# GpSimd rounds and clips half of w2, VectorE lowers it, and the orders of four engines are written anew

## The reference, cut to what matters

```python
w_down = down_project * dg[:, None] + db[:, None]        # dg, db, ug, ub from cond_512
act = relu(x @ w_down)                                    # 256 -> 64
y = act @ (up_project * ug[:, None] + ub[:, None]) + x    # 64 -> 256, the adapter's output
def bitlinear(x, w, b): return act_quant(rmsnorm(x)) @ weight_quant(w).T + b
out = x + bitlinear(gelu(bitlinear(y, w1, b1)), w2, b2)   # 256 -> 1024 -> 256
# weight_quant: s = 1 / clip(mean|w|); clip(round(w * s), -1, 1) / s
# act_quant:    s = 127 / clip(max|x|); clip(round(x * s), -128, 127) / s
```

## Time and profile before

| what | value |
|---|---|
| time, median of 3 runs | 84.02 us (83.64 to 84.12) |
| the profiled execution's own time | 84.57 us |
| its span, first to last instruction | 82.9 us |
| around the span | 1.67 us |
| granted TensorE clock | 1.0 of full speed |
| busy time, share of the span: PE | 68.6 us, 83% |
| VectorE | 71.6 us, 86% |
| ScalarE | 65.3 us, 79% |
| GpSimd | 44.1 us, 53% |

### The profile page before, as it was taken

One profiled execution on the slowest core, in us unless ns is written; L12 is line 12 of the kernel. 1 busy time (PEld: TensorE's weight loads), 2 busy tenths in 40 slices (PEclk: granted clock), 3 DMA queues, 4 the chain that ended last, 5 costly groups with the idle time before them and its releaser, 6 DMA issues.

```text
span 82.9 us, 1692 instructions
## 1 busy us (share of the span) xinstructions
PE 68.6 (83%) x507; PEld 39.9 (48%) x507; DVE 71.6 (86%) x153; ACT 65.3 (79%) x127; POOL 44.1 (53%) x113
## 2 busy tenths in 40 slices
PE   4989717599799449899999999999999999948740
PEld 1533215034354134376666594484765662836730
DVE  2158859999899999999999999989999989999950
ACT  0601198838899997969999999999999999999600
POOL 6800007856459989970078183079604872975140
PEclk9999999999999999999999999999999999999999
DMA  0887999999300000000030200300030030002033
GB/s 26 260 296 265 405 342 425 427 415 382 125 4 4 0 12 0 4 0 0 0 126 9 116 11 0 127 0 8 0 127 0 0 127 0 12 21 106 0 127 127
DMA packets 3212, 9.18 MB, mean 111 GB/s; under 512 B 370, under 2 KB 882, under 8 KB 2820
## 3 DMA queue, kind: packets, MB, share of 16 engines
q1 hardware_dynamic: 3168, 9.05, 28.9%
q10 hardware_dynamic: 36, 0.04, 0.1%
HBM read 6.98 MB, written 2.10 MB: 110 GB/s over the span
## 4 chain that ended last, share of the span: by engine, by line
PE 42%; DVE 23%; DMA 10%; issue 8%; POOL 6%; ACT 4%; SPq 3%; DVEq 1%; POOLq 0%; ACTq 0%
PE out_ps L347 11%; DMA w<-w_t 10%; PE h L309 10%; DVE mx L650 7%; PE q2t_ps L333 6%; PE up_ps L279 5%; PE h L316 4%; DVE q L691 4%; DVE w2q L823 2%; POOL rms L1024 2%; PE out_ps L345 2%; PE q2t_ps L290 2%; DVE step L659 2%; DVE y L738 2%; DVE mx L655 2%
## 5 line engine op out<-in xcount | busy, mean ns | idle before, releaser
L650 DVE TENSOR_REDUCE mx<-g 128x1 f32<-128x1024 f32 x16 | 19.4, 1210 | 0.5 <-ACT g L513 0.3
L513 ACT ACTIVATE g<-h,deq 128x1024 f32<-128x1024 f32 x16 | 18.2, 1137 | 0.2 <-PE h L316 0.2
L521 ACT ACTIVATE junk<-g,sq_scale 128x1024 bf16<-128x1024 f32 x15 | 17.5, 1172 | 0.0
L309 PE MATMUL h<-w1q,q1t 128*128 128x512 f16 x64 | 16.0, 380 | 1.5 <-ACT q1t L537 1.5
L347 PE MATMUL out_ps<-w2q,q2t 128*128 128x256 f16 x112 | 14.4, 273 | 0.0
L691 DVE TENSOR_SCALAR q<-g,m 128x1024 f32<-128x1024 f32 (+1 forms) x16 | 13.1, 825 | 0.1
L1009 POOL TENSOR_TENSOR var<-ms,eps_w 128x2 f32<-128x2 f32 (+1 forms) x10 | 2.8, 278 | 19.4 <-ACT junk_y L531 10.1
L347 PEld LDWEIGHTS out_ps<-w2q,q2t 128*128 128x128 f16 x112 | 10.9, 98 | 1.6 <-issue 0.3
L993 POOL TENSOR_TENSOR xx<-xx,b 128x512 f32<-128x512 f32 x8 | 10.1, 1273 | 1.7 <-DMA b<-b_rows 1.6
L548 ACT ACTIVATE q2t<-q2t_ps 128x512 f32<-128x512 f32 x16 | 9.9, 617 | 1.4 <-PE q2t_ps L333 1.4
L333 PE MATMUL q2t_ps<-ident,q 128*128 128x128 f16 x128 | 9.7, 220 | 1.4 <-DVE q L691 1.4
(11 more groups left out here) (109 smaller groups left out, 113.2 us busy)
## 6 DMA issues: line engine op xcount, KB each, us to landing
xx<-x_both SPq DMA_DIRECT2D x3, 1024.0 KB, 14.0
w<-w_t SPq DMA_DIRECT2D x4, 512.0 KB, 9.3
out<-xx SPq DMA_DIRECT2D x7, 256.0 KB, 2.0
xx<-x_both SPq DMA_DIRECT2D x2, 256.0 KB, 4.9
xx<-x_both SPq DMA_DIRECT2D x1, 512.0 KB, 9.3
upk<-up_pack SPq DMA_DIRECT2D x1, 384.0 KB, 3.5
out<-xx SPq DMA_DIRECT2D x2, 128.0 KB, 1.8
dpk<-down_pack SPq DMA_DIRECT2D x1, 129.0 KB, 2.1
```

The costliest lines, as they stand in the source:

```text
L309: pe.matmul(h[s][:, cols], q1t[:, j % 2, s, c, :], w1q[:, c, cols], start=(c == 0), stop=False)
L513: a.activation(g[:, j % G_RING, s, :], h[s][:, :], ACT.Gelu, scale=deq[:, col:col + 1])\
L521: a.activation(junk[:, j % 2, s, :], g[:, j % G_RING, s, :], ACT.Square, scale=sq_scale[:, 0:1], accum_out=ms[:, col:col + 1]).then_inc(gs ...
L650: v.tensor_reduce(mx[:, col:col + 1], g[:, j % G_RING, s, :], AX.X, ALU.max, apply_absolute_value=True)\
```

## The change

The first two rounding steps of w2's half 1 go from ScalarE to GpSimd, in the order round, clip, and VectorE lowers the clipped half to float16 where it clipped it before:

```diff
-            def round_w2():        # ScalarE
-                a.wait_ge(iws_ready, 2)
-                a.activation(w2_half[1], w2_half[1], ACT.Identity, bias=round_col[:, 0:1], scale=iws[:, 0:1])\
-                    .then_inc(w2_rounded[1], 1)
-            def lower_w2():        # ScalarE
-                a.wait_ge(w2_rounded[1], 1)
-                a.activation(w2q_half[1], w2_half[1], ACT.Identity, bias=neg_round[:, 0:1]).then_inc(w2_low[1], 1)
+            def lower_second_w2():  # VectorE
+                v.wait_ge(w2_low[1], 1)
+                v.tensor_scalar(w2q_half[1], w2_half[1], -ROUND, None, ALU.add).then_inc(w2_ready[1], 1)
+            def round_w2():        # GpSimd
+                p.wait_ge(iws_ready, 2)
+                p.tensor_scalar(w2_half[1], w2_half[1], iws[:, 0:1], ROUND, ALU.mult, ALU.add).then_inc(w2_rounded[1], 1)
+            def clip_w2():         # GpSimd
+                p.wait_ge(w2_rounded[1], 1)
+                p.tensor_scalar(w2_half[1], w2_half[1], ROUND + 1.0, ROUND - 1.0, ALU.min, ALU.max).then_inc(w2_low[1], 1)
```

The lists of calls are new on TensorE, ScalarE, VectorE and GpSimd. GpSimd's, whole:

```diff
+            weight_constants(0)
             first_scales()
             first_weight_scale()
             inverse_parts(0)
-            weight_constants(0)
             dequantisers(-1)
+            weight_constants(1)
             inverse_scale(1)
             inverse_parts(1)
-            add_b2(0)
+            round_w2()
             dequantisers(0)
-            weight_constants(1)
-            add_b2(1)
             inverse_scale(2)
             inverse_parts(2)
-            add_b2(2)
-            add_b2(3)
+            clip_w2()
             dequantisers(1)
             inverse_scale(3)
             inverse_parts(3)
+            add_b2(0)
             dequantisers(2)
             inverse_scale(4)
             inverse_parts(4)
+            add_b2(1)
+            add_b2(2)
             dequantisers(3)
             inverse_scale(5)
             inverse_parts(5)
+            add_b2(3)
+            add_b2(4)
             dequantisers(4)
-            add_b2(4)
             inverse_scale(6)
             inverse_parts(6)
+            add_b2(5)
+            add_b2(6)
             dequantisers(5)
             inverse_scale(7)
             inverse_parts(7)
-            add_b2(5)
+            add_b2(7)
             dequantisers(6)
-            add_b2(6)
-            add_b2(7)
             dequantisers(7)
             dequantisers(8)
```

VectorE's, up to w2 and at its end (the middle is reordered in the same manner):

```diff
             scale_down()
+            split_b1(0)
             shift_down()
             scale_up()
             shift_up()
-            split_b1(0)
+            split_b1(1)
             add_x(0)
...
             add_x(1)
-            split_b1(1)
+            abs_sum_w2()
             largest_y(1)
+            total_weights(1)
             first_steps(-1)
+            weight_scale(1)
             first_multipliers(-1)
+            inverse_weight_scale(1)
             quantise_y(1)
-            abs_sum_w2()
+            round_w2()
             largest_g(0, 0)
             add_x(2)
-            total_weights(1)
+            largest_g(0, 1)
             largest_y(2)
+            add_x(3)
...
             square_last()
             combine(6, 1)
             combine(6, 0)
+            combine(7, 1)
             combine(7, 0)
-            combine(7, 1)
```

TensorE's, up to the first pair: `weight_sum(1)` goes ahead of `add_bias(0, 0)`, `down(3)`, `up(3)` to `up(5)` come earlier and `sum_w2` later, and in the last pairs slot 1 goes ahead of slot 0:

```diff
             up(0)
-            keep_busy(6)
+            keep_busy(8)
             weight_sum(0)
             down(1)
             transpose_q1(0)
-            keep_busy(3)
+            keep_busy(2)
             up(1)
+            keep_busy(2)
             first_layer(0, 0)
             transpose_inv(0)
             first_layer(0, 1)
+            weight_sum(1)
             add_bias(0, 0)
             down(2)
+            add_bias(0, 1)
             transpose_q1(1)
-            add_bias(0, 1)
             up(2)
-            weight_sum(1)
+            down(3)
+            up(3)
+            transpose_inv(1)
             first_layer(1, 0)
```

More of the change, by code:

```diff
@@ L375, in _ @@
             first_layer(0, 1)
+            weight_sum(1)
             add_bias(0, 0)
             down(2)
+            add_bias(0, 1)
             transpose_q1(1)
-            add_bias(0, 1)
             up(2)
-            weight_sum(1)
+            down(3)
+            up(3)
+            transpose_inv(1)
             first_layer(1, 0)
+            add_bias(1, 0)
+            up(4)
+            transpose_q2(0, 0)
             first_layer(1, 1)
-            transpose_inv(1)
-            down(3)
-            add_bias(1, 0)
             add_bias(1, 1)
-            transpose_q2(0, 0)
-            up(3)
+            transpose_q2(0, 1)
             transpose_q1(2)
-            sum_w2()
-            up(4)
+            up(5)
             transpose_inv(2)
             first_layer(2, 0)
-            transpose_q2(0, 1)
             add_bias(2, 0)
@@ L399, in _ @@
             add_bias(2, 1)
-            second_layer(0, 1)
+            sum_w2()
             transpose_q1(3)
-            up(5)
-            second_layer(0, 0)
-            transpose_q2(1, 1)
+            down(4)
             transpose_inv(3)
             first_layer(3, 0)
+            second_layer(0, 0)
+            add_bias(3, 0)
+            second_layer(0, 1)
             first_layer(3, 1)
-            add_bias(3, 0)
-            second_layer(1, 0)
-            second_layer(1, 1)
+            transpose_q2(1, 1)
             transpose_q2(2, 0)
-            down(4)
             add_bias(3, 1)
-            transpose_q2(2, 1)
             up(6)
             transpose_q1(4)
-            second_layer(2, 0)
-            second_layer(2, 1)
+            second_layer(1, 1)
             transpose_inv(4)
+            second_layer(1, 0)
+            first_layer(4, 1)
+            transpose_q2(2, 1)
+            add_bias(4, 1)
             first_layer(4, 0)
@@ L876, in _ @@
             first_multipliers(0)
-            inverse_weight_scale(1)
+            second_multiplier(0)
             quantise_first(0)
+            quantise_second(0)
+            add_x(4)
             quantise_y(2)
-            round_w2()
-            largest_g(0, 1)
+            largest_g(1, 0)
+            largest_y(3)
             lower_w2()
-            second_step(0)
+            first_steps(1)
+            largest_y(4)
+            first_multipliers(1)
             clip_w2(0)
-            clip_w2(1)
@@ L886, in _ @@
[L886 to L893, removed]
             quantise_first(1)
-            add_x(4)
+            lower_second_w2()
+            add_x(5)
             quantise_y(3)
             largest_g(1, 1)
+            copy_w2_sums()
+            largest_g(2, 0)
             second_step(1)
+            first_steps(2)
@@ L899, in _ @@
             second_multiplier(1)
-            largest_y(4)
+            first_multipliers(2)
             quantise_second(1)
[L902 to L906, removed]
             largest_g(2, 1)
             quantise_first(2)
+            combine(0, 0)
             second_step(2)
-            add_x(5)
+            quantise_y(4)
+            combine(0, 1)
             second_multiplier(2)
-            quantise_y(4)
+            largest_g(3, 0)
@@ L913, in _ @@
+            largest_y(5)
+            largest_g(3, 1)
+            first_steps(3)
             quantise_second(2)
+            first_multipliers(3)
             combine(1, 0)
             combine(1, 1)
[L916 to L919, removed]
+            second_step(3)
+            quantise_first(3)
+            quantise_y(5)
+            second_multiplier(3)
             add_x(6)
-            quantise_first(3)
-            largest_g(3, 1)
@@ L923, in _ @@
[L923 to L927, removed]
             quantise_second(3)
+            largest_g(4, 1)
             largest_y(6)
@@ L931, in _ @@
             first_steps(4)
+            combine(2, 1)
+            combine(2, 0)
+            first_multipliers(4)
+            second_step(4)
             add_x(7)
-            first_multipliers(4)
-            largest_g(4, 1)
             quantise_first(4)
-            second_step(4)
+            second_multiplier(4)
             largest_y(7)
-            second_multiplier(4)
+            quantise_second(4)
             quantise_y(6)
-            quantise_second(4)
-            combine(3, 1)
[L942 to L950, removed]
-            quantise_y(7)
-            combine(4, 0)
[L953 to L957, removed]
+            largest_g(5, 0)
+            largest_g(5, 1)
+            combine(3, 0)
+            first_steps(5)
+            second_step(5)
+            first_multipliers(5)
+            second_multiplier(5)
+            quantise_first(5)
+            quantise_second(5)
+            combine(3, 1)
+            quantise_y(7)
+            largest_g(6, 1)
+            largest_g(6, 0)
+            second_step(6)
+            combine(4, 1)
+            second_multiplier(6)
+            first_steps(6)
+            combine(4, 0)
             first_multipliers(6)
-            second_multiplier(6)
+            quantise_second(6)
```

(8 more changed lines are left out.)

92 lines of the change are left out of this document (45 added, 47 removed).

## The result

The changed kernel takes 80.59 us (median of 4 runs, 80.38 to 80.92) against 84.07 us of the kernel before in the same series: a ratio of 0.958, 95% interval 0.950 to 0.966. I had forecast 83.9 and a range of 82.0 to 85.5. That my forecast was 0.1 us under the kernel before says nothing for it, since 0.1 is less than a measurement can tell. The direction is that of my first rival, but the gain of 3.5 us is more than twice its 1.6. The profiled execution of the changed kernel took 80.55 us, with a span of 78.8.

What follows compares the result with a forecast made beforehand. VectorE was taken as the bound: +0.27 - 0.68 + 0.75 - 0.8 + 0.4 = -0.06 us, rounded to -0.1, put on the median of 84.02 gave 83.9 us; range 82.0 to 85.5.

Steps and rivals of the forecast that it cites:

- my first rival: VectorE's standing still beside GpSimd's wide operations falls to the late rate: -1.6 us, 82.4 us; chance 0.30.
- the pricing of GpSimd's wide operations: VectorE's standing still beside b2's additions and w2's passes: 2.6 us against 3.4, so -0.8 (-2.0 to +3.9).
- the account: From 12.9 to 80.6 us VectorE works 64.76 of 67.7 us, so terms add up there; other engines only limit gains.
- slack of about 2.4 us: ScalarE loses w2 passes of 1.24 and 1.14 us; not the fullest engine, so this alone gives nothing.
- Lowering for clip: On VectorE, w2's second half: a float16 clip (0.42) goes, a lowering (0.69) comes: +0.27 us.
- GpSimd's passes: GpSimd gains two one-input passes of 128x1024 float32 over w2, taken at 1.1 us each.
- The start: GpSimd's constants start the scales 0.65 us later; VectorE waits 1.15 us for w2's sum: +0.75 net (0.1 to 1.6).
- split_b1: The second split of b1 leaves VectorE's full stretch at 16.61 us for a place before add_x(0): -0.68 us.
- The stores: At the end, both last stores issue behind VectorE's last combination: +0.4 us, covered by nothing.
- the one for being wrong: Sign in the profile after: VectorE's excess durations under 1.5 us or over 3.5 would refute the forecast.
- ScalarE's time without work: Sign in the profile after: ScalarE's idle time up by 1 to 2 us would confirm the forecast.

Runs made afterwards that it cites:

- e2: The changed kernel without GpSimd's eight additions of b2 (output lacks b2): 80.65 us, ratio 0.964 to the kernel before.
- e10: The changed kernel with only the first addition of b2 moved up behind dequantisers(0): 81.16 us, ratio 0.974 to the kernel before.
- e1: The kernel before without GpSimd's eight additions of b2 (output lacks b2): 82.3 us, ratio 0.983.
- e4: The changed kernel with rounding and lowering of w2's second half back on ScalarE, its clip on VectorE: 82.71 us, ratio 0.986 to the kernel before.
- e5: The kernel before with w2's second half rounded and clipped on GpSimd and lowered on VectorE, no order changed otherwise: 86.74 us, ratio 1.039.
- e8: The changed kernel with GpSimd's first constants back behind the first inverse parts: 79.39 us, ratio 0.950 to the kernel before.
- e14: The changed kernel with the second split of b1 back behind add_x(1), run beside a control: 81.09 us, ratio 0.969 to the kernel before.
- e9: The changed kernel with the second split of b1 back behind add_x(1): 80.78 to 84.77 us in six runs, ratio 0.977 to the kernel before.
- e7: The changed kernel with SyncE waiting for slot 1 ahead of slot 0 for the last two stores: 79.99 us, ratio 0.957 to the kernel before.
- e3: The kernel before with only b2's additions moved to their places in the changed kernel: 85.57 to 87.16 us, ratio 1.023.
- the version with both edits: The changed kernel with first constants behind the first inverse parts and last stores waiting for slot 1 first: 79.01 us, ratio 0.946 to the kernel before.

## Why the prediction was wrong

The step that failed is the pricing of GpSimd's wide operations: "I take 0.3 each, 2.4, and 0.2 for both w2 passes". They cost VectorE nothing (e2, and no excess in the profile after). The term was -0.8 and should have been about -3.8, which is outside its own bounds (-2.0 to +3.9): I had bounded an addition below by the mean of the late four, where nothing excluded that it costs nothing. I had the mechanism, saw that the first four cost 0.67 and the last four 0.18 (0.27 with the two that I missed), and then averaged over unknown places, though the new lists were there to be walked through. e2 and e10 show how wrong an average is here: by the place alone one addition costs nothing or 0.8 to 1.4 us.

The second step that failed is the account: "VectorE is therefore the account in which I add up the change". That account is right only as long as VectorE bounds. e1 against e4 shows it: without the standing still but with w2 on ScalarE, the old orders give a ratio of 0.983 and the new ones 0.986, nearly the same, and ScalarE is busy for 41.85 and 42.00 of 42 us in the two. The remaining 1.9 us come from taking w2 off ScalarE, an edit that I put at nothing ("slack of about 2.4 us") and that costs 3.2 us when it is made alone (e5). The gain has two parts: additions out of the way 1.4, and the passes on GpSimd 1.9 on top, the latter only in orders that have a place for them. Together they are 3.3 us, beside the 3.5 and 3.0 that the two series of the changed kernel show.

The other terms:

- *Lowering for clip*, +0.27: by duration 0.68 and 0.39 after for a pair of 0.85 before, +0.22. Right.
- *GpSimd's passes*, 1.1 us each: 1.12 and 1.04. Right. The estimate of 0.88 from the Trainium skill (GPSIMD Engine Reference, section 3.1) is 21 and 15% below the two rows. The Trainium skill's rule (the same page, section 4.1) that this work belongs on VectorE did not hold for this kernel's time, where VectorE and ScalarE are full and GpSimd was not.
- *The start*, VectorE waits 1.15 us for the sum. The timeline of the changed kernel:

```profile
19.45 0.16 DVE L772 TENSOR_REDUCE wsum<-out_ps 128x1 f32<-128x2 f32 x1 [1.14 <-PE out_ps L272]
```

  The wait is right to 0.01, but partly by luck. I took each constant at its short duration and let the scales start 0.65 later; in fact the two constants take 1.42 us beside VectorE's passes and the scales start 1.76 later (14.68 instead of 12.92), and then the operations behind them are shorter than before (the power 0.79 us instead of 1.41, the last one 0.23 instead of 0.54), so that the parts are ready only 0.64 later. The wait was not priced in full, as ScalarE waits for the same inverses and bounds later on: its wait before `copy_invt(0)` rose from 1.53 to 2.25, and putting the constants back (e8) lowers it to 1.21 and wins 0.7 to 1.2 us.
- *split_b1*, -0.68: gone from VectorE's account, but in the new order it would have lain in part in the wait that the constants make. e14 gives 0.4, not 0.7, and e9 more; the size stays open.
- *The stores*, +0.4. After and then e7, SyncE's timelines:

```profile
76.21 0.81 SPq L225 DMA_DIRECT2D out<-xx  x2
```

```profile
75.61 0.82 SPq L225 DMA_DIRECT2D out<-xx  x2
```

  In the changed kernel the first of the two issues after VectorE's last instruction (ends 76.18), in e7 it issues 0.36 before that one ends (75.97). The span behind VectorE's end falls from 2.6 to 2.2 us. Right in size, though e7's times alone don't show it.

With the one term put right, these sum to +0.2 + 0.75 - 0.68 + 0.4 - 3.8 = -3.1 on VectorE's account. That this is near the 3.5 measured is luck: e1 takes away the same 3.8 us and gains 1.4. VectorE's busy time fell by some 1 us more than the excess, the split and the clip explain. Most of that is a closer overlap of neighbouring instructions: from 12.9 us on, the sum of their durations exceeds the busy time by 8.0 us in the kernel before and by 8.8 in the changed one.

Of the signs that I had named, the one for being wrong came (an excess under 1.5 us), and so did VectorE's wait, the passes' durations and the place of the stores. ScalarE's time without work, which I had rising by 1 to 2 us, fell from 6.6 to 4.9.

## What to carry to other kernels

Look for the time in which an instruction stands still inside its own duration: compare its duration with the same form elsewhere, and look at what GpSimd did at that moment. Look at both engines: when one no longer stands still, the other may do so instead. Where three engines are full together, a relief of one is worth less than its size (1.4 of 3.8 us in e1) until the others are relieved too, so each edit alone (e1, e3, e5) says little of the two together. When a list of calls decides what stands beside what, walk the new list in time instead of taking an average price for each call.

## What the runs showed of the hardware

The standing still goes both ways, as GpSimd's constants and its power of 1.56 us in the changed kernel show above. In e14 the split of b1 on VectorE (0.73 us from 16.05, two inputs in SBUF) stands beside GpSimd's step `rest<-std,iws` of two columns, which takes 0.56 where it takes 0.20 in the changed kernel, and TensorE's wait for the inverses rises from 1.19 to 1.55 us:

```profile
16.28 0.56 POOL L1038 TENSOR_TENSOR rest<-std,iws 128x2 f32<-128x2 f32 x1
```

The Trainium skill (SBUF — State Buffer, section Who interferes with whom) names both directions, and row maxima as never blocked: the trace of the changed kernel agrees, with 2.5 us of additions beside maxima of undisturbed 1.2 us. Who comes first can't be read from starts this close: in the kernel before, the quantisation at 23.68 is listed 0.03 us ahead of the addition at 23.71 and was still the one that stood.

In e9's profile TensorE stood idle for 1.55 us before 19.57 and then ran at a granted clock of 0.50, which is 1.2 GHz, from 21 to 25 us:

```profile
17.00:21.00 4.00, 2.45 (x10) 1.05 (x11) 3.02 (x5) 1.39 (x6) 2.06 (x10) 0.86 0.86 354
21.00:25.00 4.00, 4.00 (x20) 1.88 (x19) 2.91 (x9) 2.10 (x5) 3.01 (x11) 0.50 0.04 14
```

e14, the same kernel with the same wait of 1.55 us, kept the full clock in its profile. Whether the wait caused the fall isn't settled by this one profile; in the version with both edits, that wait of TensorE is gone.
